# Two state space scans inside a 12-stage network on one core: another order of the steps within a scan round

## The chip, the cores and the metric

One core of a Trainium2 chip runs the whole program. The metric is the device time of one execution in microseconds (us), the median of a few runs. The engines are TensorE (PE in the profile; its weight loads are PEld), VectorE (DVE), ScalarE (ACT), GpSimd (POOL) and SyncE (SP, which only issues transfers). Each engine runs its own list of instructions strictly in the order in which the program issues them, and waits on semaphores where it needs another engine's result.

## The reference, cut to what matters

The network has 12 stages over 1024 tokens of width 256. Two of them are state space blocks ("Mamba 2"); the larger one, `ssd3`, has 64 heads of 64 channels and the smaller, `ssd2`, 8 heads. Cut to its core:

```
proj = hidden @ in_proj_w                       # x, gate z, B, C, dt
x, B, C = silu(causal_conv4(proj_xBC))          # 4 taps per channel
cum   = cumsum(dt * A)
decay = exp(mask(cum_i - cum_j))
scores = (C_i . B_j) * decay * dt_j
Y_diag = scores @ x
state  = chunk_decay * state + B^T (decay_to_end * dt * x)
Y_off  = (C @ state) * exp(cum)
y = (Y_diag + Y_off + D * x) * silu(z)
out = (y * rsqrt(mean(y*y) + eps) * norm_w) @ out_proj_w
```

## The kernel before

The kernel is one program in which each engine walks through the same list of steps, `order[si]`, stage by stage, and issues of every step only its own part. For the two scan stages `ssd_order` writes that list. The work of a scan stage is cut into units. A job is a group of 8 heads (512 channels) with one of two sequences; a job has 4 units, one for each chunk of 128 tokens. So `ssd3` has 16 jobs and 64 units, and `ssd2` has 2 jobs and 8 units. The list is software pipelined: in round r each step of the tuple `ROUND` (L2378) handles unit n = r - lag. Rounds run from -9 to N + 8. Steps such as `silu`, `scan`, `xd` and `scale` come once in 4 rounds. The change is in the order of that tuple alone, so it alters the order inside a round on each engine.

What the steps that matter here do, and on which engine (n is the unit):

- `wo` (lag 3): TensorE, 8 matmuls 128x256, the output projection; `add`: VectorE adds it to `yacc`.
- `E` (lag 0): TensorE, two matmuls that use strips of 32 rows of the array (the exponents' strip products), and, for three chunks in four, the full-array product `EC`. `decay`: ScalarE takes Abs of both `E` banks, Exp of the tile, and Exp of `EC`. `mask`: VectorE multiplies the tile with the masked C.B products.
- `S` (lag 1): TensorE, the products `off` (8 matmuls 128x128) and `S` (2 of 128x512). `state`: VectorE reads both.
- `y` (lag 1): TensorE, 16 matmuls into strips of 64 columns (the outputs' strip products); it needs the masked tile of its unit. `merge`: VectorE adds the result.
- `conv` and `z` (lag -7): TensorE, 6 matmuls 128x512 each, the two input projections. For `conv`, ScalarE copies the bank with one tap and VectorE adds three taps; for `z`, ScalarE copies the bank.
- `xt` and `xt0`: TensorE, 4 transposes, and ScalarE's copy of them. `xt` runs in three rounds out of four, `xt0` in one.
- `scan` (lag -5, once in 4 rounds): ScalarE writes `dA4` in two small copies, TensorE multiplies it (2 matmuls 128x128, bank `cumT`), ScalarE reads the bank three times, then VectorE and GpSimd go on.
- `silu` (lag -3, once in 4 rounds): ScalarE, two passes over 128x2048. `split` (lag -8): ScalarE and VectorE split the next weights, in every second job. `square`, `gate`, `sum`, `keep`, `x`: ScalarE (square) and GpSimd.

PSUM has 8 banks of 128x512 f32. `Psum.take` deals them out in the order in which TensorE takes them: bank k is the one that was taken 8 takes earlier, and TensorE first waits for that one's last reader. So the order of the tuple also decides whose reader each take waits for. The takes are `wo` 1, `E` 2, `EC` 1, `cumT` 1, `off` 1, `S` 1, `conv` 1, `y` 1, `z` 1, `xt` or `xt0` 1. A round has 8 to 11 of them.

A round is named here by r modulo 4, as r0, r1, r2 and r3. `silu` comes in r1, `xt0` in r2 (where the normal `xt` comes too), `scan` in r3, `xd` (4 scalings of the converted tile on ScalarE) in r0. r0 has no `EC` and no `S`; r1 has no `off` and no `xt`.

Lines: L79 is `Engine.mm`, L83 `Engine.tr`, L87 `Engine.act`, L91 `Engine.tt`, L99 `Engine.stt`, L111 `Engine.copy`; all of them are helpers, so groups are told apart by tiles and shapes. All buffers of the scan are cut from the large tiles `wt`, `work`, `ering`.

Of the kernel before, what the change touches and what calls it, by code (L numbers as in the profile page):

```python
# [200 lines left out]
def build(nc, D, out):  # L201
    ctx = ExitStack()
    with ctx:
# [2171 lines left out]
        SSD["ssd3"] = ssd_buffers("ssd3", 4096, 64)  # L2375
        s_xz, s_wo = [sig(f"xz_in{i}") for i in range(8)], [sig(f"wo_in{i}") for i in range(2)]

        ROUND = (("add", 3), ("wo", 3), ("E", 0), ("gate", 2), ("state", 1), ("x", 0), ("scan", -5), ("keep", 0), ("S", 1), ("xt0", -2), ("decay", 0), ("merge", 1), ("conv", -7), ("silu", -3), ("split", -8), ("scale", -1), ("sum", 2), ("square", 2), ("y", 1), ("z", -7), ("mask", 0), ("xd", 0), ("xt", -3))  # L2378
        LEAD = {-9: [("dt",), ("softplus",), ("bc", 0, 0), ("dA",)], -8: [("bc", 1, 0), ("bc", 0, 1)],
                -7: [("cum",)], -5: [("ready",)], -4: [("bc", 1, 1)], 0: [("bc", 0, 2), ("bc", 1, 2)]}  # L2380

        def ssd_order(si):
# [11 lines left out]
            for r in range(-9, N + 9):  # L2394
                todo.extend(LEAD.get(r, ()))
                for step, lag in ROUND:
                    n = r - lag
# [781 lines left out]
```

How the kernel before makes its waits and increments, by code:

```python
    def wait_ge(self, signal, *label):  # L57
        value = signal.at[label] if label and self.sure else signal.at.get(label, 0) if label else signal.n
        if value > self.seen.get(signal, 0):
            self.seen[signal] = value
            self.e.wait_ge(signal.sem, value)
# [103 lines left out]
    def take(self, pe, *key):  # L165
        k = len(self.order)
        b = Bank(k, self.aps[k % 8])
        self.order.append(b)
        self.uses[key] = b
        if k >= 8 and len(self.old) > k:
            assert self.old[k - 8].readers
            for signal, value in self.old[k - 8].readers:
                if value > pe.seen.get(signal, 0):
                    pe.seen[signal] = value
                    pe.e.wait_ge(signal.sem, value)
        return b.ap
# [175 lines left out]
        def need_hT(pe, si, tiles):  # L352
            for t in tiles:
                pe.wait_ge(hT_by(t), "hT", si, t)
# [1 line left out]
        def v_norm(v, step, si, t):  # L356
            if step == "na":
                if si:
                    v.wait_ge(V, "X", si - 1, t)
                else:
                    v.wait_ge(s_x, "X", t // HALF)
                v.bn(lst[:, t, :], X[:, t, :]).then_inc(V)
                v.wait_ge(V)
                v.bn_end(lmv[:, t, :], lst[:, t, :]).then_inc(V, "mv", si, t)
            elif step == "nb":
                v.wait_ge(A, "sd", si, t)
# [20 lines left out]
        def pe_norm(pe, step, si, t):  # L387
            if step == "turn":
                b = ps.take(pe, "turn", si, t)
                pe.wait_ge(V, "H", si, t)
                for c in range(2):
```

## Time and profile before

| what | value |
|---|---|
| median of 3 runs | 1964.95 us (1962.99 to 1966.03) |
| span of the profiled execution | 1943.9 us |
| outside the span (median less span) | 21.05 us |
| PE busy in the span | 1691.9 us (87%) |
| DVE busy | 1457.5 us (75%) |
| ACT busy | 1222.1 us (63%) |
| POOL busy | 891.9 us (46%) |
| mean granted TensorE clock | 0.926 of full speed |

The span runs from the first to the last instruction. The page gives no separate device time for the profiled execution; the difference to the median of the runs, 21.05 us, is what lies around the span and is taken as constant. `ssd2` lies between about 900 and 985 us of the span and `ssd3` between about 1195 and 1808 us. Inside `ssd3` the full rounds, in which all steps are present, lie between about 1270 and 1740 us.

### The profile page before, as it was taken

The page shows a single profiled execution, that of the slowest core. Times are in us where ns is not written, and L with a number is a line of the kernel's source. Part 1 is how long each engine was busy: PE and PEld are TensorE (multiplying, and loading weights), DVE is VectorE, ACT ScalarE, POOL GpSimd, SP SyncE. Part 2 cuts the span into 40 slices and gives each one's busy share as a digit, 9 for nine tenths or more (in the row PEclk, how much of TensorE's full clock was granted, in tenths as well). Part 3 has the DMA queues.
Part 4 walks back from the last instruction along what each step waited for, and adds up shares of the span by engine and source line. Part 5 has one row for each costly group of instructions (what it writes and reads, how often), then busy time and mean ns, then how long its engine had stood idle before and what let it go on. Part 6 is the DMA issues. An engine that isn't in the chain of part 4 may idle for free. (4 is left out here: it accounts for less than half of the span.)

```text
span 1943.9 us, 29621 instructions
## 1 busy us (share of the span) xinstructions
PE 1691.9 (87%) x10866; PEld 1350.1 (69%) x10866; DVE 1457.5 (75%) x3045; ACT 1222.1 (63%) x2463; POOL 891.9 (46%) x870
## 2 busy tenths in 40 slices
PE   6899579979994667798878998899999999997899
PEld 4799257858992356696667886667777777775788
DVE  7888687577886766686677667678788888877576
ACT  4587247646871269317932544888988989887443
POOL 0775541107856300301722220267788787878321
PEclk9999789989996779798989998999999999999799
DMA  8797214117973100000020100000100000000111
GB/s 306 230 294 241 66 55 150 51 35 235 295 228 92 60 1 2 1 1 0 1 97 1 37 30 1 23 12 22 34 17 23 28 23 20 25 14 1 45 49 36
DMA packets 74605, 139.86 MB, mean 72 GB/s; under 512 B 11476, under 2 KB 52564, under 8 KB 73428
## 3 DMA queue, kind: packets, MB, share of 16 engines
q1 hardware_dynamic: 63700, 108.50, 16.9%
q0 software_dynamic: 10752, 29.37, 5.3%
q8 instruction: 89, 1.46, 0.3%
q14 instruction: 64, 0.52, 0.1%
HBM read 113.72 MB, written 24.12 MB: 71 GB/s over the span
## 5 line engine op out<-in xcount | busy, mean ns | idle before, releaser
L79 PE MATMUL ps<-H_r,wt_r 128*128 128x512 f32 (+1 forms) x732 | 284.6, 429 | 11.7 <-ACT wt L87 4.7
L79 PE MATMUL ps<-work_r 128*128 128x256 f32 (+2 forms) x1200 | 248.0, 297 | 6.7 <-DVE work_r L91 2.6
L87 ACT ACTIVATE work<-ps 128x512 f32<-128x512 f32 (+3 forms) x354 | 168.1, 498 | 120.4 <-PE ps L79 103.3
L91 DVE TENSOR_TENSOR work<-work,ps 128x512 f32<-128x512 f32 (+4 forms) x304 | 170.7, 562 | 90.9 <-ACT work L87 57.6
L79 PE MATMUL ps<-wt,work 128*128 128x256 f32 (+1 forms) x1120 | 221.0, 372 | 20.4 <-POOL work L91 10.0
L99 DVE SCALAR_TENSOR_TENSOR wt<-ps,wt 128x511 f32<-128x511 f32 (+2 forms) x234 | 174.3, 747 | 47.2 <-ACT wt L87 41.1
L79 PEld LDWEIGHTS ps<-work_r 128*128 128x128 f32 (+1 forms) x1200 | 189.8, 187 | 28.6 <-DVE work_r L91 11.4
L79 PEld LDWEIGHTS ps<-wt,work 128*128 128x128 f32 (+1 forms) x1120 | 168.4, 201 | 44.6 <-ACT work L87 10.0
L79 PEld LDWEIGHTS ps<-H_r,wt_r 128*128 128x128 f32 (+1 forms) x732 | 139.8, 191 | 63.0 <-issue 14.5
L91 POOL TENSOR_TENSOR work<-work 128x256 f32<-128x256 f32 (+2 forms) x160 | 131.8, 827 | 108.1 <-ACT work L87 87.6
L87 ACT ACT_TABLE_LOAD x113 | 145.0, 1283 | 47.7 <-DVE lmv L119 29.2
L79 PE MATMUL ps<-hT_r,wt_r 128*128 128x512 f32 (+1 forms) x432 | 172.6, 400 | 0.0
L79 PE MATMUL ps<-ering_r,work_r 128*128 128x256 f32 (+1 forms) x742 | 163.5, 301 | 0.9 <-ACT work L87 0.9
L145 POOL DMA_INDIRECT work<-Hd,work x128 | 123.4, 964 | 88.4 <-DVE work L123 58.3
L79 PE MATMUL ps<-ering,work 128*64 128x128 f32 (+2 forms) x1600 | 149.9, 288 | 7.8 <-DVE ering L91 4.0
L79 PEld LDWEIGHTS ps<-ering,work 128*64 128x64 f32 (+1 forms) x1600 | 124.9, 155 | 44.6 <-issue 18.5
L87 ACT ACTIVATE work_r<-work 48x256 fp32r<-48x256 f32 (+1 forms) x200 | 99.1, 495 | 77.8 <-DVE work L91 71.4
L79 PE MATMUL ps<-wt,hT 128*128 128x8 f32 (+4 forms) x384 | 110.4, 433 | 34.3 <-ACT hT L87 17.6
L145 POOL DMA_INDIRECT ering<-ye,get x96 | 94.4, 984 | 92.4 <-DVE X L99 42.2
L91 POOL TENSOR_TENSOR work<-wt,work 128x512 f32<-128x512 f32 x112 | 134.7, 1220 | 0.0
L87 ACT ACTIVATE wt<-wt 128x512 f32<-128x512 f32 (+4 forms) x152 | 132.1, 934 | 2.5 <-DVE wt L99 2.2
L99 DVE SCALAR_TENSOR_TENSOR X<-ps,work,X 128x256 f32<-128x256 f32 x256 | 114.4, 478 | 18.2 <-PE ps L79 11.6
(255 smaller groups left out, 4203.0 us busy)
## 6 DMA issues: line engine op xcount, KB each, us to landing
ering<-in_moe_w SPq DMA_DIRECT2D x87, 624.0 KB, 5.8
ye<-work SPq DMA_DIRECT2D x64, 256.0 KB, 4.6
wt<-in_ssd_wg SPq DMA_DIRECT2D x64, 128.0 KB, 2.2
ye<-early SPq DMA_DIRECT2D x1, 4096.0 KB, 14.6
wt<-in_ssd_wg SPq DMA_DIRECT2D x8, 512.0 KB, 3.6
Hd<-H SPq DMA_DIRECT2D x16, 128.0 KB, 1.7
wt<-in_ret_fc SPq DMA_DIRECT2D x2, 1024.0 KB, 11.7
work<-Hd,work POOLq DMA_INDIRECT x128, 4.8
```

The lines of the kernel that those rows point to most:

```text
L79: self.last = self.e.matmul(o, l, r, start=start, stop=stop, skip_group_check=True)
L87: self.last = self.e.activation(o, a, f, **kw)
L91: self.last = self.e.tensor_tensor(o, a, b, op)
L99: self.last = self.e.scalar_tensor_tensor(out=o, in0=a, scalar=s, in1=b, op0=op0, op1=op1, **kw)
L145: self.last = self.e.indirect_dma_start(out=out, out_offset=at(out_off), in_=in_, in_offset=at(in_off))
```

## The change

One tuple is reordered; no step, lag, instruction or transfer is added or taken away.

```diff
--- before.py
+++ after.py
@@ -2375,7 +2375,7 @@
-        ROUND = (("add", 3), ("wo", 3), ("E", 0), ("gate", 2), ("state", 1), ("x", 0), ("scan", -5), ("keep", 0), ("S", 1), ("xt0", -2), ("decay", 0), ("merge", 1), ("conv", -7), ("silu", -3), ("split", -8), ("scale", -1), ("sum", 2), ("square", 2), ("y", 1), ("z", -7), ("mask", 0), ("xd", 0), ("xt", -3))
+        ROUND = (("wo", 3), ("gate", 2), ("x", 0), ("scan", -5), ("keep", 0), ("S", 1), ("xt0", -2), ("add", 3), ("state", 1), ("y", 1), ("square", 2), ("E", 0), ("merge", 1), ("decay", 0), ("mask", 0), ("conv", -7), ("silu", -3), ("split", -8), ("scale", -1), ("sum", 2), ("z", -7), ("xd", 0), ("xt", -3))
```

Read engine by engine, the order in a round becomes:

| engine | before | after |
|---|---|---|
| TensorE | wo, E, EC, scan, off, S, xt0, conv, y, z, xt | wo, scan, off, S, xt0, y, E, EC, conv, z, xt |
| ScalarE | scan, xt0, decay, conv, silu, split, scale, square, z, xd, xt | scan, xt0, square, decay, conv, silu, split, scale, z, xd, xt |
| VectorE | add, state, scan, merge, conv, split, mask | scan, add, state, merge, mask, conv, split |
| GpSimd | gate, x, scan, keep, sum | gate, x, scan, keep, sum |
| SyncE | transfers after conv and z, after wo | the same |

## Rows read from the trace of the kernel before

**Rows 1.** Windows view, full rounds of `ssd3`: length, busy time per engine, granted clock, DMA.
```profile
1270.00:1750.00 480.00, 472.25 (x2830) 344.77 (x2828) 396.69 (x541) 424.18 (x690) 376.25 (x378) 1.00 0.08 22
```

**Rows 2.** Timeline of PE, one round r2: start, busy, engine, line, operation, tiles, count.
```profile
1400.33 1.89 PE L79 MATMUL ps<-wt,work 128*128 128x256 f32 x8
1402.15 0.50 PE L79 MATMUL ps<-ering_r,wt_r 32*128 32x512 f32 x2
1402.58 0.50 PE L79 MATMUL ps<-work_r 128*128 128x512 f32 x1
1402.91 1.05 PE L79 MATMUL ps<-ering,work 128*128 128x128 f32 x8
1403.80 1.02 PE L79 MATMUL ps<-work,ering 128*128 128x512 f32 x2
...
1405.79 0.50 PE L79 MATMUL ps<-H_r,wt_r 128*128 128x512 f32 x1 [0.53 <-ACT wt L87]
...
1407.59 1.09 PE L79 MATMUL ps<-ering,work 128*64 128x128 f32 x16
1408.61 0.50 PE L79 MATMUL ps<-H_r,wt_r 128*128 128x512 f32 x1
1408.95 0.40 PE L79 MATMUL ps<-hT_r,wt_r 128*128 128x512 f32 x1
...
1410.11 0.60 PE L83 MATMUL ps<-cst,wt 128*128 128x128 f32 x4
1410.54 0.81 PE L79 MATMUL ps<-wt,work 128*128 128x256 f32 x3
```

**Rows 3.** Timeline of PE, two sequences rare before: S then y, y then E.
```profile
930.54 1.97 PE L79 MATMUL ps<-ering,work 128*64 128x128 f32 x16 [2.65 <-DVE ering L91]
932.44 0.79 PE L79 MATMUL ps<-ering_r,wt_r 32*128 32x512 f32 x2
...
1741.35 1.02 PE L79 MATMUL ps<-work,ering 128*128 128x512 f32 x2
1742.30 1.09 PE L79 MATMUL ps<-ering,work 128*64 128x128 f32 x16
```

**Rows 4.** Timeline of PE, landmarks: z of r0 thrice, E, scan of r3, E.
```profile
1356.49 0.50 PE L79 MATMUL ps<-H_r,wt_r 128*128 128x512 f32 x1
...
1390.63 0.50 PE L79 MATMUL ps<-H_r,wt_r 128*128 128x512 f32 x1
...
1394.41 0.50 PE L79 MATMUL ps<-ering_r,wt_r 32*128 32x512 f32 x2
...
1413.26 0.46 PE L79 MATMUL ps<-cst,work 128*128 128x128 f32 x2
...
1421.57 0.49 PE L79 MATMUL ps<-ering_r,work_r 32*128 32x512 f32 x2
...
1425.75 0.50 PE L79 MATMUL ps<-H_r,wt_r 128*128 128x512 f32 x1
```

**Rows 5.** Timeline of ACT: decay of r1, dA4 of r3, in two jobs, and between.
```profile
1361.61 1.07 ACT L87 ACTIVATE ering<-ps 128x512 f32<-128x512 f32 x2
...
1377.32 0.42 ACT L87 ACTIVATE work<-work 128x64 f32<-128x64 f32 x2
...
1395.78 1.08 ACT L87 ACTIVATE ering<-ps 128x512 f32<-128x512 f32 x2
...
1404.64 0.61 ACT L87 ACTIVATE work<-work 128x512 f32<-128x512 f32 x1
1405.17 1.06 ACT L87 ACTIVATE wt<-ps 128x512 f32<-128x512 f32 x2
...
1412.70 0.41 ACT L87 ACTIVATE work<-work 128x64 f32<-128x64 f32 x2
...
1422.09 1.08 ACT L87 ACTIVATE ering<-ps 128x512 f32<-128x512 f32 x2 [1.50 <-PE ps L79]
```

**Rows 6.** Timeline of DVE, the three taps of one `conv`.
```profile
1375.98 2.32 DVE L99 SCALAR_TENSOR_TENSOR wt<-ps,wt 128x511 f32<-128x511 f32 x3 [1.55 <-ACT wt L87]
```

## The prediction

> **What bounds the kernel now.** I read the windows view first, because the change touches only the scan stages. In the 480 us of full rounds TensorE is busy 472.25 us, at full clock, while ScalarE has 424.18 us and VectorE 396.69 us [rows 1]. So TensorE is the bound on average, with ScalarE 12% behind it. The average does not say how the slack is spread, so I then read the PE timeline of one round, measuring from the start of one group to the start of the next [rows 2], and last the ACT timeline over a whole job of four rounds [rows 4, 5].
>
> The PE timeline shows two kinds of loss. The first is paid at each passage between full-array products and strips. In [rows 2] `wo` to `E` takes 1.82: eight matmuls at 0.216 (seven of them lie between 1400.33 and the last start, 1.89 less its own 0.38) would make 1.73, so entering strips costs 0.09. Leaving the `y` strips costs 0.10 before `z` (`y` to `z` takes 1.02) and another 0.10 inside `z`: its first matmul is followed after 0.34, the others at 0.232 ((1410.11 - 1408.95) / 5), so `z` takes 1.50, where six at 0.232 are 1.39.
>
> The second loss is a true wait: `conv` of r2 starts at 1405.79 after 0.53 idle, released by ScalarE [rows 2]. It takes the bank of `z` of r1, eight takes back, and ScalarE copies that bank only at 1405.17, behind `silu` [rows 5]. ScalarE is saturated over this stretch: from Abs of r1 at 1395.78 to `dA4` at 1412.70 its operations follow each other, and the scan product starts at 1413.26, 0.56 after `dA4` [rows 4, 5]. The `E` of that r1 had been issued at 1394.41, 1.37 before ScalarE came to it: before the change ScalarE does not wait for `E` in r1. It does wait in r0, 1.50 us for the `E` issued at 1421.57 [rows 4, 5].
>
> **The change, part by part.** No instruction comes or goes, so only passages and waits count.
>
> *Passages.* `E` now follows `y`, not `wo`: minus 0.09. `z` now follows `conv`, not `y`: minus 0.20. The passage from `y` strips to `E` strips is new. The nearest case is at half clock, where `E` starts 0.07 before the end shown for the 16 `y` matmuls (930.54 + 1.97 against 932.44) [rows 3]; `z` behind `y` at full clock also starts 0.07 before it (1407.59 + 1.09 against 1408.61) [rows 2]. So I charge the same 0.10; bounds 0 to 0.20. `S` to `y` takes 0.95 [rows 3], which is 2 x 0.43 plus the 0.09 that `conv` to `y` paid before. Net per full round: -0.19 us, 56 rounds: -10.6 us, if TensorE alone set the pace.
>
> *ScalarE's chain.* It starts `decay` of r1 only when `E` is there, and `E` now comes later in the round, behind `S` and `y`. I count from the start of `z` in r0. TensorE needs `z` 1.39 + `xt` 0.43 + `wo` 1.73 + `S` 0.95 + `y` 1.02 = 5.52 to `E` [rows 2, 3]; Abs starts 0.52 after it (1422.09 - 1421.57) [rows 4, 5]: 6.04. Before, Abs of r1 started 5.15 after `z` (1395.78 - 1390.63). ScalarE loses 0.89, in which it now does one `square` (0.52, from 1404.64 to 1405.17) that formerly stood later.
>
> From Abs to the scan product the chain was 17.48 (1413.26 - 1395.78) in a job with `split`; less that `square` it is 16.96. In a job without `split` ScalarE needed 15.71 (1377.32 - 1361.61) to `dA4`, plus 0.56 less 0.52: 15.75 [rows 4, 5]. TensorE by itself would need about 14.3 from `E` of r1 to the scan product of r3: `E`, `EC`, `conv`, `z` 3.55; in r2 `wo`, `off`, `S` and transposes 3.48, strip entry and `y` 1.6, `E`, `EC`, `conv`, `z`, `xt` 3.98; `wo` 1.73 [rows 2, 3]. ScalarE's chain is 0.52 + 16.96 = 17.5 or 16.3. So TensorE, which formerly had another `y` and another `E` with `EC` in this stretch, waits 2 to 3 us in it: about 1 us at `EC` of r2, which now takes the bank of `z` of r1 (eight takes back), and up to 2 us at the scan product. Behind that waiting product are `off`, `S`, `y` and `E` of r3, so all of the round shifts; a wait at `EC` itself is followed by `conv` and `z`.
>
> *From the scan product to the next `z` of r0*, TensorE runs in its own time; ScalarE is idle before both `decay` steps there. In the new order: scan 0.30, `off` 0.89, `S` 0.95, `y` 1.02, `E` 0.43, `EC` 0.34, `conv` 1.39, `z` 1.39, `xt` 0.43, `wo` 1.73, `off` with strip entry 0.98, `y` 1.02, `E` 0.43, `conv` behind strips 1.49, together 12.79 [rows 2, 3, 4].
>
> *Sum of one job.* With `split` 6.04 + 16.96 + 12.79 = 35.79, against 35.12 before (1425.75 - 1390.63): +0.67. Without, 6.04 + 15.75 + 12.79 = 34.58, against 34.14 (1390.63 - 1356.49): +0.44 [rows 4]. There are 14 such periods, 7 of each kind: **+7.8 us**. If `y` to `E` is free, `E` of r1 comes 0.10 earlier and the last stretch is 0.20 shorter: +3.6. If it costs 0.20: +12.
>
> *VectorE.* `mask` moves ahead of the taps, so it idles behind `merge` until Exp is done, with the taps (2.32) [rows 6] and `split` queued behind. The bank takes that wait for taps are `EC` of r1 and the second `E` bank of r2; followed through the job, taps end about 0.8 us before either. `y` needs `mask` one round later and has some 2 us left. I charge 0.
> *GpSimd and SyncE* keep their order; transfers are issued behind the same steps. 0.
>
> *Fill and end of both scans.* Without `conv` and `z`, `E` stands behind `off`, `S` and `y`, 0.89 + 0.95 + 1.02 = 2.86 later in its round, and `square` stands before `decay` in the chain of the last rounds, 0.52 each in some three rounds per scan. Bounds: 0, if ScalarE is busy anyway, as in r1 before; 2 x 2.86 if the last `E` of both scans is late in full. I take +2.
>
> **Forecast.** Span 1943.9 + 7.8 + 2 = 1953.7; with the 21.05 around it 1974.8, say **1975 us**, 0.5% slower. Its own range is 1969 to 1981.
>
> **The rivals.** *Passages win.* If ScalarE keeps ahead after all, the -10.6 stand and the time is 1954. For it speaks that TensorE is 98% busy [rows 1]. Against it: it requires the chain from Abs of r1 to the scan product to be 2 to 3 us shorter than it was, and nothing is taken out of it but one `square`. The Trainium skill, TensorEngine Tiling (Array Packing), section Tiling Modes, says that changing the tiling mode drains the engine; by that rule three changes of mode a round in place of four are a gain, and the page gives no figure. By it alone the time would be this rival's. Chance 0.15.
>
> *The two cancel.* ScalarE's lag is half of what I count, for instance because `E` of r1 comes before ScalarE is free there, as before the change. The chain is then 0.5 us shorter per period, and with it goes the end of the stages: +7.8 - 14 x 0.5 = about +1, 1966. Chance 0.2.
>
> *VectorE becomes a second wait.* If `mask` in front of the taps makes them miss the 0.8 us that I find, each period gets a wait of 1 to 2.3 us (the taps themselves [rows 6]) at a bank: +14 to +32 instead of the chain's share, 1983 to 1997. It decides if taps start over 0.8 us later than the mask's end allows. Chance 0.1.
>
> The main case has 0.55. The waits could also lower the clock; the granted clock was 1.00 through the waits before [rows 1], so I give that no share of its own.
>
> **How the numbers follow.** About 0.2% (3.9 us) is what a measurement of this kernel can tell from no change. Slower: nearly all of 0.55 and all of 0.1, 0.62. Same: 0.2 and the low end of the main case, 0.23. Faster: 0.15. The range 1955 to 1985 reaches from the passages' rival to the near end of VectorE's; it holds the main case and the cancelling one.
>
> **What would show it.** In the changed profile: `y` to `E` in 1.02 and `conv` to `z` in 1.39 (passages right); Abs of r1 waiting for TensorE, which it did not before; a wait of about 1 us at `EC` of r2 and one of 1.5 to 2 us at the scan product of r3, both released by ScalarE; ScalarE without idle time between; jobs of 35.8 and 34.6 us. PE busy in the full rounds falls from 98% to about 93%, and the clock stays at full speed. The forecast is wrong if ScalarE is not late at the scan product, or if the long waits are released by VectorE.

## The result and the profile after

| | median | against the kernel before, same chip |
|---|---|---|
| before | 1965.49 us (1962.99 to 1969.46, 4 runs) | |
| changed | 1988.53 us (1984.98 to 1991.76, 4 runs) | 1.0115, 95% interval 1.0102 to 1.0128 |
| changed, second time | 1988.6 us (5 runs; before 1968.64) | 1.0104, 1.0086 to 1.0122 |

The change costs 1.0 to 1.15%, 20 to 23 us. The forecast was 1975, so the sign is right and the size is half of the truth; the time lies above the range.

The windows view of the changed kernel shows its `ssd2`, the 14 full jobs of `ssd3`, a job with `split` and one without (columns as in [rows 1]):

```profile
895.70:1027.20 131.50, 107.10 (x547) 80.21 (x548) 87.30 (x161) 93.47 (x171) 55.81 (x57) 0.84 0.00 1
1279.61:1780.77 501.16, 460.35 (x2827) 349.98 (x2826) 398.33 (x544) 430.67 (x701) 373.81 (x376) 1.00 0.07 20
1351.36:1388.27 36.91, 33.23 (x204) 25.18 (x203) 29.69 (x42) 31.76 (x53) 27.26 (x27) 1.00 0.07 22
1388.27:1422.83 34.56, 32.95 (x205) 25.19 (x203) 26.62 (x37) 29.55 (x48) 26.06 (x27) 1.00 0.09 24
```

The same view of the kernel before, over its `ssd2` and its 14 full jobs:

```profile
871.70:999.20 127.50, 103.48 (x548) 76.39 (x548) 85.90 (x161) 93.74 (x171) 54.88 (x57) 0.88 0.00 1
1250.93:1736.80 485.87, 474.14 (x2828) 345.70 (x2826) 397.66 (x543) 431.35 (x702) 372.12 (x375) 1.00 0.07 21
```

TensorE is busy 14 us less in the same matmuls, and the stretch is 15.3 us longer: cheaper passages, and more waiting than they save. (The clock is full in both but for one stretch of 3.40 us in the first of the 14 jobs before the change, where it is at 0.50 with TensorE busy throughout; by an estimate from that row, 1.7 us of the 14 are this.) ScalarE, VectorE and GpSimd do the same work in the same time to 2 us. A job without `split` takes 34.56 (34.58 predicted), one with `split` 36.91 (35.79 predicted). The whole miss inside `ssd3` is in the jobs with `split`.

The PE timeline of that job and the next, at the places where TensorE waits (columns as in [rows 2]):

```profile
1355.85 1.09 PE L79 MATMUL ps<-ering,work 128*64 128x128 f32 x16
1356.87 0.50 PE L79 MATMUL ps<-ering_r,wt_r 32*128 32x512 f32 x2
1357.31 0.50 PE L79 MATMUL ps<-work_r 128*128 128x512 f32 x1
...
1366.91 0.50 PE L79 MATMUL ps<-work_r 128*128 128x512 f32 x1 [0.72 <-ACT wt L87]
...
1374.38 0.46 PE L79 MATMUL ps<-cst,work 128*128 128x128 f32 x2 [1.62 <-ACT work L87]
...
1385.22 0.49 PE L79 MATMUL ps<-ering_r,work_r 32*128 32x512 f32 x2
1386.81 0.47 PE L79 MATMUL ps<-H_r,wt_r 128*128 128x512 f32 x1 [1.10 <-DVE wt_r L91]
...
1410.05 0.46 PE L79 MATMUL ps<-cst,work 128*128 128x128 f32 x2 [1.43 <-DVE wt L99]
```

The first three rows are the new sequence `y`, `E`, `EC`: 1.02 and 0.44. Then come `EC` of r2, the scan product of r3, `E` and `conv` of r0, and the scan product of the next job. The first two waits are forecast. The third is not: `conv` of r0 starts 1.59 after `E` (1386.81 against 1385.22), where the natural distance is 0.43. (The releaser named at 1410.05 is the last one by the record; that the `dA4` copies hold it is shown by `d_after` below.)

Where this wait comes from is best seen in the chain of waits, followed back from `z` of that r0 (start, time, engine and tile):

```profile
1374.38 3.71 PE ps L79 x30
1378.09 1.08 ACT ering L87 x2
1379.17 0.02 issue
1379.20 1.07 ACT ering L87
1380.27 0.02 issue
1380.29 2.02 DVE ering L91
1382.31 0.67 DVE wt L99
...
1384.53 2.14 DVE wt_r L91 x2
1386.67 0.14 issue
1386.81 2.99 PE ps L79 x12
```

From the scan product the path runs through `off`, `S`, `y`, `E`, then Abs, Exp, `mask`, the taps and the two `split` operations, and only then `conv`. `conv` of r0 needs the weights that `split` of r3 writes. This is a data wait (`pe.wait_ge(V, "split", ...)`), not a bank. Before the change `mask` was last in its round. The DVE and PE timelines of the kernel before, `split` of r3 and `conv` of r0:

```profile
1421.73 1.29 DVE L91 TENSOR_TENSOR wt_r<-wt,wt_r 128x256 fp32r<-128x256 f32 x2
```
```profile
1423.17 0.47 PE L79 MATMUL ps<-H_r,wt_r 128*128 128x512 f32 x1
```

`split` ended at 1423.02 and `conv` began 0.15 later. That is already some 0.2 us late: from scan product to `conv` it took 9.91 us in this job (1413.26 to 1423.17) and 9.68 in the one without `split` ahead of it (1378.36 to 1388.04). So this wait stood in the trace before, with no slack left, and could have been read there.

The grouped DVE view (1270 to 1740 us) shows where VectorE now stands: group, count, busy, mean ns, idle before. First the changed kernel, then the kernel before:

```profile
L91 DVE TENSOR_TENSOR ering<-ering 128x1024 f32<-128x1024 f32 x52 | 83.4, 1604 | 63.9 <-ACT ering L87 63.9
```
```profile
L91 DVE TENSOR_TENSOR ering<-ering 128x1024 f32<-128x1024 f32 x55 | 84.0, 1528 | 0.0
```

VectorE now stands idle for 63.9 us in front of `mask`, and for none before the change. All that follows `mask` in its list starts that much later.

The stages, between the same matmuls (by their number) in each trace, in us:

| kernel | `ssd2` | `ssd3` fill | full rounds | end |
|---|---|---|---|---|
| before | 127.5 | 58.7 | 488.6 | 98.1 |
| changed | 131.5 | 59.4 | 503.8 | 97.1 |
| changed, second time | 134.2 | 58.6 | 503.7 | 98.6 |
| `d_after` | 128.0 | 56.8 | 485.2 | 96.2 |
| `d_after_split` | 127.9 | 56.8 | 476.9 | 97.2 |
| `b_mix` | 122.9 | 54.0 | 479.2 | 99.1 |
| `d_before` | 122.8 | 53.7 | 490.4 | 96.2 |
| `c_gscan` | 131.6 | 59.5 | 496.7 | 95.7 |

Everything between the two scans and behind them is alike to 1.2 us. The stretch ahead of `ssd2` took 871.7 us in the profile of before and 891 to 897 in these others, but 871 to 875 in the first four experiments below, taken on a chip on which the kernel before runs in 1946.6. So it goes with the chip and not with the change.

### The profile page after: what moved, and what is told of

Read it like the earlier page. It is cut to its first block and busy times, and to the rows that moved or that the text cites. A ratio compares the mean times of both kernels' runs of the same rounds, so it can differ in the third digit from the quotient of the medians.

```text
span 1987.5 us, 29653 instructions
## 1 busy us (share of the span) xinstructions
PE 1694.8 (85%) x10866; PEld 1366.9 (69%) x10866; DVE 1457.4 (73%) x3045; ACT 1221.9 (61%) x2463; POOL 891.5 (45%) x870
## 3 DMA queue, kind: packets, MB, share of 16 engines
q8 instruction: 90, 1.47, 0.3%
## 5 line engine op out<-in xcount | busy, mean ns | idle before, releaser
L79 PE MATMUL ps<-H_r,wt_r 128*128 128x512 f32 (+1 forms) x732 | 259.0, 406 | 15.4 <-DVE wt_r L91 11.7
L91 DVE TENSOR_TENSOR ering<-ering 128x1024 f32<-128x1024 f32 (+4 forms) x90 | 119.5, 1328 | 103.9 <-ACT ering L87 103.4
L91 POOL TENSOR_TENSOR work<-work 128x256 f32<-128x256 f32 (+2 forms) x160 | 143.1, 900 | 72.8 <-DVE work L91 30.7
L87 ACT ACTIVATE work_r<-work 48x256 fp32r<-48x256 f32 (+1 forms) x200 | 99.1, 496 | 80.0 <-DVE work L91 73.5
L79 PE MATMUL ps<-wt,hT 128*128 128x8 f32 (+4 forms) x384 | 111.0, 434 | 37.7 <-DVE hT L111 13.9
L87 ACT ACTIVATE lrs<-lmv,epsc 128x1 f32<-128x1 f32 x96 | 27.8, 294 | 172.1 <-DVE lmv L119 136.2
## 6 DMA issues: line engine op xcount, KB each, us to landing
wt<-in_ssd_wg SPq DMA_DIRECT2D x64, 128.0 KB, 2.2
Hd<-H SPq DMA_DIRECT2D x16, 128.0 KB, 1.7
```

Source lines behind the costliest of these rows:

```text
L79: self.last = self.e.matmul(o, l, r, start=start, stop=stop, skip_group_check=True)
L87: self.last = self.e.activation(o, a, f, **kw)
L91: self.last = self.e.tensor_tensor(o, a, b, op)
```

## The experiments

My theory after the first result: two lags cause the loss. ScalarE is late at the scan product of r3 in every job (as forecast), and VectorE is late at `conv` of r0 in the jobs with `split`, because `mask`, which waits for the late `E`, stands ahead of the taps and `split`. The rivals: the late `E` alone, or the clock. All edits are to the changed kernel unless said. Where an expectation gives a time, it is meant for a chip on which the kernel before takes 1965.5 us; the first four runs are from a faster one, and there the ratio is what compares.

**`e_front`: `E` back behind `wo`, all else in the new order.**

```diff
-ROUND = (("wo", 3), ("gate", 2), ... ("square", 2), ("E", 0), ("merge", 1), ...
+ROUND = (("wo", 3), ("E", 0), ("gate", 2), ... ("square", 2), ("merge", 1), ...
```

> The changed kernel with one step put back: E and EC stand behind wo again (y stays ahead of conv, mask stays ahead of the taps). My theory: what costs time is that E comes late, because ScalarE's decay and VectorE's mask wait for it. Then a job without split takes 34.1 us and one with split 34.7 to 35.1, and the time is 1961 to 1967 us, level with the kernel before. The rival, that y ahead of conv (its bank now comes from z of the round before, its mask is needed earlier) is what costs: the time stays at 1983 or more.

Measured: 1954.59 against 1946.62, ratio 1.0033 (1.0019 to 1.0047), some 15 us better than the change. By the ratio it is 1972 us where 1961 to 1967 were expected. Jobs of 35.1 and 34.5: the waits at the scan product and at `conv` of r0 are gone, and the split job is back at its old time. The job without `split`, expected at its old 34.1, is 0.4 above it: `y` of r2 waits 0.32 for the bank of `z` of r1 and `wo` of r3 0.35, both released by ScalarE (0.90 and 0.36 in a job with `split`). The place of `E` carries most of the loss.

**`e_mask_back`: `mask` behind `z`, as it was.**

```diff
-... ("decay", 0), ("mask", 0), ("conv", -7), ... ("z", -7), ("xd", 0), ...
+... ("decay", 0), ("conv", -7), ... ("z", -7), ("mask", 0), ("xd", 0), ...
```

> The changed kernel with mask put back to the end of VectorE's round, behind conv's taps and split. My theory of the second loss is that split on VectorE stands behind mask, and conv of r0 waits for split of r3. Then that wait of about 1.1 us in jobs with split goes away (scan product to next z of r0 12.8 us instead of 13.9). But y stands early now and needs mask: I expect y to wait 0.5 to 1 us in r0 and r1 of each job and up to 4 us in r2 of jobs with split, so 1990 to 2010 us in all. The rival, that mask ahead of the taps is pure loss: 1980 or less.

Measured: 2048.7, ratio 1.0511 (1.049 to 1.0533), which is 2066 us by the ratio: far above the 1990 to 2010 expected. Jobs of 36.2 and 46 us. PE timeline, `y` in two neighbouring rounds:

```profile
1435.71 1.09 PE L79 MATMUL ps<-ering,work 128*64 128x128 f32 x16 [1.67 <-DVE ering L91]
...
1448.21 1.73 PE L79 MATMUL ps<-ering,work 128*64 128x128 f32 x16 [3.63 <-DVE ering L91]
```

With `y` early in the round, `mask` cannot stand late: `y` waits for it, and the late `y` makes the next `E` and so the next `mask` late. The expectation had the direction; it missed that the waits feed each other and that the clock falls too. The granted clock over the 14 jobs is 0.93 (1.00 in the changed kernel), and the second `y` above takes 1.73 in place of 1.09. From scan product to `z` the jobs take 14.3 and 18 to 19, not the 12.8 expected, so this run does not show what the wait for `split` is worth. It does show that the early `mask` is not an avoidable part of the change.

**`e_split_first`: `split` ahead of `decay` and `mask`.**

```diff
-... ("merge", 1), ("decay", 0), ("mask", 0), ("conv", -7), ("silu", -3), ("split", -8), ...
+... ("merge", 1), ("split", -8), ("decay", 0), ("mask", 0), ("conv", -7), ("silu", -3), ...
```

> The changed kernel with split moved ahead of decay on ScalarE and so ahead of mask on VectorE. My theory: VectorE's split is then done while it would idle before mask, the wait at conv of r0 in jobs with split goes (13.9 to 12.8 us), and one split (0.6 us) leaves ScalarE's chain between Abs of r1 and the scan product: jobs with split fall from 37.0 to 35.3 us, jobs without stay at 34.6. 7 x 1.7 = 12 us less than the changed kernel: 1975 to 1979 us. The rival, that the 1.1 us comes from a bank (taps of r3) and not from split: at most 0.6 us a job is gained, 1984 us.

Measured: 1961.97, ratio 1.0068 (1.0052 to 1.0084). The first two split jobs take 35.78 and 35.23, with 12.78 and 12.77 from scan product to `z`: the wait at `conv` is gone. They were expected at 35.3; from the third on they take 37.2 again, for another reason. PE timeline and windows of such a place:

```profile
1491.24 0.46 PE L79 MATMUL ps<-cst,work 128*128 128x128 f32 x2 [2.08 <-ACT work L87]
1491.54 1.23 PE L79 MATMUL ps<-ering,work 128*128 128x128 f32 x8
1492.56 1.92 PE L79 MATMUL ps<-work,ering 128*128 128x512 f32 x2
1494.41 1.70 PE L79 MATMUL ps<-ering,work 128*64 128x128 f32 x16
```
```profile
1485.00:1492.29 7.29, 5.21 (x30) 4.30 (x29) 4.56 (x6) 6.62 (x15) 3.82 (x5) 1.00 0.00 0
1492.29:1495.70 3.41, 3.41 (x17) 1.91 (x18) 2.66 (x6) 1.55 (x5) 0.00 (x0) 0.50 0.00 0
```

`split` now stands ahead of `decay` on ScalarE, the scan product waits 2.08 in place of 1.62, and behind it the granted clock is at 0.50 (1.2 GHz) for 3.41 us. This happens in the last five split jobs, with waits of 2.04 to 2.08; the second one waits 2.04 too and keeps its clock. In the changed kernel, with 1.6 in six split jobs and 1.9 in the first, it stays at 1.00 through all jobs. The rival that put the split jobs' loss on the clock is out for the changed kernel, but the clock is what ate this experiment's gain: its 14 jobs take 499.1 us, 2.0 less than with the change. By the ratio the time is 1979 us, at the end of the 1975 to 1979 expected, but not by the mechanism expected: the jobs fall by 2 us of the 12, and the medians, taken on two chips, differ by 7 to 9. Differences of this size between the two chips I leave open.

**`o_ssd2`: the new order in `ssd2` alone, the old in `ssd3`.**

```diff
-for step, lag in ROUND:
+for step, lag in (NEW if q.key == "ssd2" else OLD):
```

> The new order in the small scan stage alone, the old order in the large one. From the two traces I read 4 us for the small stage and 15 for the large one: 1969 to 1970 us. If the small stage's share is an accident of the two profiled executions: 1965 to 1966 us.

Measured: 1949.98, ratio 1.0019 (1.0005 to 1.0033): 3.7 us. `ssd2` goes from 127.5 to 131.4, as expected. The 14 full jobs of `ssd3`, in the old order, take 487.8 in place of 485.9: in four of the split jobs `conv` of r0 waits 0.3 for `split`, which takes 1.61 there where it takes 1.28 in a job without this wait, and they take 35.38 in place of 35.04. So the wait for `split` can show in the old order too, only smaller. PE timeline of the changed kernel in `ssd2`:

```profile
979.07 1.09 PE L79 MATMUL ps<-ering,work 128*64 128x128 f32 x16 [1.05 <-DVE ering L91]
...
986.64 1.09 PE L79 MATMUL ps<-ering,work 128*64 128x128 f32 x16 [1.51 <-DVE ering L107]
...
1002.90 1.09 PE L79 MATMUL ps<-ering,work 128*64 128x128 f32 x16 [1.85 <-DVE lrs L107]
```

Each of these starts 0.09 to 0.15 after the end of a `mask` (978.92, 986.49 and 1002.81); the short operations named as releasers in the last two follow `mask` on VectorE. With no `conv` and `z` left to run in the meantime, `y` stands behind `E`, Exp and `mask` in full.

**`r_after` and `r_before`: ScalarE relieved.** Both leave out the `silu` of z, one of the two 1.9 us passes of r1 (the gate then multiplies with z itself); one on the new order, one on the old.

```diff
-a.act(q.sz[j % q.nx], q.sz[j % q.nx], ACT.Silu).then_inc(A, "sz", si, j)
+a.mark("sz", si, j)
```

> The changed order with ScalarE relieved: the silu of the gate z is left out (the gate multiplies with z itself), so one pass of 1.8 us is gone from ScalarE's chain of every job. My theory: the chain from Abs of r1 to the scan product sets the pace in the changed order, so its jobs shrink by most of 1.8 us: without split from 34.6 to 32.8 us, with split from 37.0 to 35.3 us. About 16 x 1.75 = 28 us less than the changed kernel: 1960 us. The rival, that TensorE or VectorE sets it: jobs stay within 0.4 us, 1983 or more.

> The same relief in the order of before. There TensorE is near its own limit (waits of about 0.7 us a job without split, 1.2 with), so only 0.5 to 1.1 us a job can be had: 33.5 and 34.2 us, in all 1950 to 1957 us. With both relieved, the order with fewer passages should come out level or ahead in jobs without split: 32.8 against 33.5 us. The rival, that passages are worth nothing in the full round: both jobs alike.

Measured: 0.9988 (0.9976 to 1.0) on the old order, and 1.0012 (0.9999 to 1.0026) on the new, which without it has 1.0104 to 1.0115. Two microseconds less on ScalarE per job are worth some 20 us in the new order and 2 in the old: ScalarE has become the limit there. Both sizes were missed. On the new order 1960 us was expected and 1968 came: the job without `split` gained 0.9 (33.65) and not 1.8, and ScalarE now idles 0.33 twice in its r2 for TensorE, at `xt0` and at `E`. On the old order 33.5 and 34.2 were expected, and the jobs stayed at 34.1 and 35.1 to 35.6. With both relieved, the new order is ahead by 0.5 in the jobs without `split`. Of the 20 us, some 4 or 5 are not ScalarE's but come from the split jobs described next.

The split jobs of `r_after` held a surprise. From scan product to `z` four of the last six take 12.77 and two 13.9 to 14.0. Windows of a short one and of a long one:

```profile
1438.70:1451.49 12.79, 12.79 (x88) 10.02 (x89) 11.84 (x20) 7.67 (x16) 9.61 (x10) 1.00 0.00 1
1575.76:1589.78 14.02, 12.83 (x88) 10.02 (x88) 13.17 (x19) 9.04 (x17) 10.82 (x12) 1.00 0.01 2
```

Then `mask`, `split` and the GpSimd operation beside `mask`, from the timelines of DVE and of POOL, first of the short one, then of the long one:

```profile
1444.62 1.23 DVE L91 TENSOR_TENSOR ering<-ering 128x1024 f32<-128x1024 f32 x1 [0.64 <-ACT ering L87]
...
1448.01 1.01 DVE L91 TENSOR_TENSOR wt_r<-wt,wt_r 128x256 fp32r<-128x256 f32 x2
...
1581.68 2.12 DVE L91 TENSOR_TENSOR ering<-ering 128x1024 f32<-128x1024 f32 x1 [0.64 <-ACT ering L87]
...
1585.94 2.22 DVE L91 TENSOR_TENSOR wt_r<-wt,wt_r 128x256 fp32r<-128x256 f32 x2
```
```profile
1444.63 2.11 POOL L91 TENSOR_TENSOR ering_r<-wt,work_r 128x512 fp32r<-128x512 f32 x1
...
1581.68 1.04 POOL L91 TENSOR_TENSOR ering_r<-wt,work_r 128x512 fp32r<-128x512 f32 x1
```

In the short one `mask` starts 0.01 ahead of GpSimd's multiply and takes 1.23, while the multiply takes 2.11. In the long one the multiply takes 1.04 and `mask` 2.12. One of the two pays about the time of the other. So it is in all 14 such places of this profile: in the four where `mask` starts at least 0.01 ahead it takes 1.23 and the multiply 2.07 to 2.11; in the other ten, from level to 0.11 behind, `mask` takes 2.02 to 2.12 and the multiply 1.04. The pair in the long one costs 2.1 us more on the path to `conv`; in the changed kernel `mask` and `split` have 2.02 and 2.21 in this place, the long form. The Trainium skill, SBUF — State Buffer, section SBUF: two separate sides, says that VectorE and GpSimd share a pair of ports under an exclusive lock, held for the whole instruction by whichever starts first, and that a VectorE operation with two SBUF inputs takes it against a GpSimd operation that reads SBUF. The rows agree, to the 0.01 that the starts tell: the loser is longer by 0.8 to 1.1, and VectorE's operations of 128x512 that read a bank keep their 0.67 to 0.69 beside a busy GpSimd.

**`d_after` and `d_before`: the scan product's input early.** The two `dA4` copies become a step of their own in r0, three rounds ahead of the product, in the new order and in the old.

```diff
-... ("y", 1), ("square", 2), ...
+... ("y", 1), ("dA4", -8), ("square", 2), ...
-            elif step == "scan":
+            elif step == "dA4":
                 four = q.dA[:, 4 * b_:4 * b_ + 4, g * 8:g * 8 + 8]
...
+            elif step == "scan":
                 b, sc = ps.of("cumT", si, j), wts["scan_c"]
```

> The changed order, with ScalarE's two small copies to dA4 moved four rounds of work earlier (lag -8, in r0, where ScalarE idles) out of the scan step. The scan product then no longer ends ScalarE's chain. My theory: its wait of 1.5 to 2 us in r3 goes, what stays is the wait at EC of r2 (0.4 to 1 us): jobs without split 33.1 us, with split 35.4 us, so about 1965 us. The rival, that the product waits for its bank or for VectorE: no change, 1985 or more.

> The same early dA4 in the order of before. There the scan product waited only 0.15 to 0.2 us beyond what the bank of conv (taps of r2) costs anyway: 0 to 2 us less in all, 1963 to 1965 us.

Measured: 0.9973 (0.9964 to 0.9983) on the new order, 26 to 28 us better than the change (18.6 of it in the 14 full jobs, 482.5 us); 0.9946 (0.993 to 0.9963) on the old. Windows of `d_before`, its 14 jobs:

```profile
1265.55:1753.16 487.61, 473.82 (x2828) 345.54 (x2826) 399.86 (x543) 430.77 (x702) 372.24 (x376) 1.00 0.07 21
```
Windows of `d_after`, a job with `split` and one without:

```profile
1411.03:1446.86 35.83, 33.28 (x205) 25.35 (x203) 30.77 (x43) 31.92 (x53) 29.61 (x30) 1.00 0.08 23
1446.86:1480.06 33.20, 32.98 (x204) 25.26 (x203) 26.13 (x37) 29.25 (x48) 26.30 (x28) 1.00 0.09 24
```

Without the wait at the scan product the job without `split` is 0.94 shorter than before the change (34.14): here the passages are cashed. The split job still waits 1.28 at `conv` of r0 for `split` (33.1 and 35.4 were expected). On the old order 0 to 2 us were expected; by the median it is 8 and by the ratio 11. It is not in the full jobs (34.12 and 35.05 to 35.38) but in `ssd2` (122.8 in place of 127.5) and in the fill of `ssd3` (53.7 for 58.7); why the two starts profit so much stays open. What matters below: the early input is worth 0.5% to the old order as well, so it is `d_before`, and not the kernel before, that the new order with early input has to beat.

**`d_after_split`: both, and `a_again`: the changed kernel on the same chip.**

> The changed order, with the two dA4 copies ahead of square in r3 and split ahead of decay. Theory (ScalarE's lag makes the scan product late, and the taps and the split standing behind mask make conv of r0 late): with both taken away the jobs keep what the passages give, 33.2 us without split and about 34.0 to 34.4 with it, against 34.15 and 35.06 of the kernel before; the changed order alone has 34.57 and 37.0. From d_after (33.2 and 35.8) the seven split jobs fall by 1.4 to 1.8 us, 10 to 12 us in all: 1 to 1.5% faster than the changed order and 0.8 to 1.1% faster than the kernel before. Rival (the split jobs lose to the clock or to ScalarE's total, not to the order of split): they stay at 35.8, and the time at d_after's 0.997 of before.

(The copies stand in r0, as in `d_after`; the expectation says r3 by mistake.)

> The changed kernel unaltered, on the same chip as the other three, so that they can be set against it: 1.0115 of the kernel before if the ratio holds from chip to chip (1.010 to 1.013). If it came out under 1.009 or above 1.014, the ratios of the other runs would have to be compared with it and not with the first result.

Measured: 1953.31 against 1968.64, 0.993 (0.9914 to 0.9946); `a_again` 1.0104 (1.0086 to 1.0122), within what was expected. For `d_after_split` 0.8 to 1.1% faster than before was expected; it is 0.7%. Windows of `d_after_split`, 14 jobs, one with `split`, one without:

```profile
1270.51:1744.78 474.27, 458.75 (x2827) 350.74 (x2826) 391.82 (x544) 426.91 (x697) 375.03 (x376) 1.00 0.08 22
1338.09:1372.40 34.31, 33.02 (x204) 25.27 (x203) 28.76 (x41) 31.02 (x52) 27.48 (x28) 1.00 0.08 23
1372.40:1405.59 33.19, 32.98 (x205) 25.27 (x203) 25.99 (x37) 29.65 (x50) 26.62 (x28) 1.00 0.09 25
```

The 14 jobs take 474.3 us, 11.6 less than before the change and 26.9 less than with it. Of the 11.6, 2.0 are in the first of them, the one that held the stretch at half clock before. The other thirteen gain 9.6, about 1.0 each without `split` and 0.4 to 0.5 with it, so the same matmul order gains about what [rows 2, 3] said the passages are worth, once the waits for ScalarE and VectorE are short. The split jobs settle at 34.6, since `conv` of r0 now waits 0.60 for the taps. In `ssd2` it still loses 5 us against `d_before` (127.9 against 122.8), so in the whole it is ahead of it by only 3 us by the ratios (0.993 against 0.9946, and the intervals overlap) and 4 by the stages.

**`b_silu`: on top of that, the `silu` of z behind the copy of z.**

```diff
+... ("z", -7), ("siluz", -3), ("xd", 0), ...
```

> As d_after_split, and the second silu pass (that of z) stands behind ScalarE's copy of z in r1, not ahead of it. Theory: the copy of z of r1 frees its bank about 3.9 us earlier, so EC of r2 no longer waits (0.2 us in a job without split, 0.8 with it in the changed order), and nothing else moves: 0.2 to 0.8 us per job, 3 to 9 us in all below d_after_split. Rival: TensorE has no wait left at EC once dA4 is early, and the pass is only moved onto the xt copy behind it: within 0.1% of d_after_split.

Measured: 0.9935 (0.9919 to 0.995), no different from `d_after_split`; the jobs are the same 33.2 and 34.6. The rival had it.

**`b_mix`: that order in `ssd3`, the old one with early `dA4` in `ssd2`.**

> ssd3 in d_after_split's order, ssd2 in the old order with the early dA4. Theory: ssd2 is short of conv and z to cover mask, so there the new order costs about 4 to 5 us (131.5 against 127.5; 128.0 against 122.8 with the early dA4) while in ssd3 it gains: about 5 us below d_after_split, 1.0 to 1.3% below the kernel before. Rival (the ssd2 difference was a difference between chips): equal to d_after_split within 0.1%.

Measured: 1945.76, 0.9889 (0.9872 to 0.9905), 1.1% faster than the kernel before, as expected, and the best of all. `ssd2` takes 122.9 in place of 127.9. Against `d_before` (0.9946) it is 11 us ahead by the ratios, and as much in the 14 jobs of `ssd3` (476.5 against 487.6): this is what the new order with `split` ahead of `decay` is worth. No run has early copies and early `split` in the old order, so the share of `split`'s new place is not shown; in the jobs without `split`, 34.12 against 33.20, it has none.

**`c_gscan`: GpSimd's multiplies of the scan out of the way.** They move from r3 to the end of r0; the PE, ACT and DVE lists are those of the changed kernel.

```diff
-... ("sum", 2), ("z", -7), ...
+... ("sum", 2), ("gscan", -4), ("z", -7), ...
-            elif step == "scan":        # g_unit
+            elif step == "gscan":
```

> The changed order, with GpSimd's three multiplies of the scan (128x256 and two 128x512) moved from r3 to the end of r0, so that in the split jobs GpSimd does not run them while VectorE's mask of r3 and its two split operations want to run. All of the data that conv of r0 waits for comes as late as before. Theory (the wait of 1.16 us at conv of r0 comes from the overlap: mask takes 2.02 us and the split pair 2.21 us there, against 1.22 and 1.01 where they run alone): mask of r3 under 1.8 us, split near 1.0, conv of r0 waits under 0.3 us, split jobs 35.8 to 36.1 instead of 37.0, no-split jobs 34.6, together 6 to 8 us or 0.3 to 0.4% below the changed kernel. Rival (the wait is the late E and Exp alone, whatever the durations): conv of r0 still waits about 1.1 us and split jobs stay at 37.0. A third outcome, that GpSimd's other operations move up into the same place and overlap as much, would show as mask and split still near 2 us, and would leave the question open.

Measured: 1980.09 against 1966.97, 1.0076 (1.0055 to 1.0097), 5 to 8 us below the changed kernel (7.1 in the 14 jobs), where 6 to 8 were expected. The split jobs take 35.92, and from scan product to `z` 12.76 us. DVE timeline, `mask` and `split` of r3, then PE at `conv` of r0:

```profile
1445.73 1.76 DVE L91 TENSOR_TENSOR ering<-ering 128x1024 f32<-128x1024 f32 x1 [0.71 <-ACT ering L87]
...
1449.64 1.33 DVE L91 TENSOR_TENSOR wt_r<-wt,wt_r 128x256 fp32r<-128x256 f32 x2
```
```profile
1450.66 0.49 PE L79 MATMUL ps<-ering_r,work_r 32*128 32x512 f32 x2
1451.12 0.47 PE L79 MATMUL ps<-H_r,wt_r 128*128 128x512 f32 x1
```

The pair takes 3.09 in place of 4.23, and `conv` follows `E` after 0.46: no wait. `E` comes as late as before. So the late `E` alone does not make the wait; it takes the late `E` and the overlap with GpSimd together. The pair did not fall to its shortest times (1.23 and 1.01 in `r_after`), since other multiplies of GpSimd moved up beside it, and `split` ends just in time (1450.97).

**`c_mix`: the same in `b_mix`.**

> As b_mix (ssd3 in the changed order with early dA4 copies and split ahead of decay, ssd2 in the old order with early dA4 copies), and in ssd3 GpSimd's scan multiplies at the end of r0. In the best order so far conv of r0 in a split job still waits 0.66 us for the taps, with mask at 1.48 and split at 1.34. Theory of the overlap: mask 1.2 to 1.3, split 1.0, the wait falls under 0.3 us, split jobs 34.2 instead of 34.6: 2 to 4 us below b_mix, 1.2 to 1.3% below the kernel before. Rival: equal to b_mix within 0.1%, 1.1% below the kernel before.

Measured: 0.9949 (0.9932 to 0.9967), 0.6% slower than `b_mix`. Both theory and rival missed. There `split` stands ahead of `mask`, and GpSimd's next two steps, moved up, fall on both: 1.84 and 2.06 in place of 1.34 and 1.48, and the split jobs take 14.7 from scan product to `z` (13.8 in `b_mix`). The jobs without `split` lose too (33.6 for 33.2). The overlap was not removed but moved.

## Why the prediction was right in sign and wrong in size

**Passages: right.** `y` to `E` takes 1.02 as charged. In a job without `split` the change is worth 0.94 us (34.14 to 33.20) where the scan product does not wait (0.87 of it in the busy time of TensorE, 33.85 to 32.98), 0.22 to 0.23 a round against the 0.19 forecast. The Trainium skill's rule that a change of tiling mode drains TensorE (TensorEngine Tiling (Array Packing), section Tiling Modes) has the sign of this right; the rival that rested on it fell by the waits.

**ScalarE's chain: right.** From `z` of r0 to the scan product 21.78 and 23.02 (1351.36 to 1374.38) were measured, where 21.79 and 23.00 had been worked out. Abs of r1 was to wait for TensorE: ScalarE idles 0.43 before it without `split`, but only 0.06 with it (`square` ends at 1357.35, Abs starts at 1357.41), so there both are late at once. The wait at the product was forecast at 1.5 to 2 and is 1.62 and 1.43, the one at `EC` of r2 at 1 and is 0.72 with `split` (0.2 without). The clock stayed full. Busy TensorE is 92% (460.35 of 501.16) for the 93% forecast.

**VectorE: the step that failed, "I charge 0".** I followed the taps to the banks that wait for them, and they are in time. I missed the other reader of VectorE's list: `split` stands behind the taps, and `conv` of r0 waits for its data. The last stretch is 12.78 without `split` (12.79 forecast) and 13.89 with it (1374.38 to 1388.27). That is 1.1 us in six split jobs and 0.8 in the first, 7.5 us, as much as the whole loss forecast for the jobs (7.8). The slack fails with it: before the change `mask` and `split` took 1.47 and 1.29 in this place, and beside GpSimd's multiplies of the scan they take 2.02 and 2.21. `c_gscan` shows that with 3.09 for the pair the charge of 0 would have held. So the missing reader alone would not have changed the forecast: with the durations read before the change `split` would have been in time. The charge fails by the reader and the longer durations together, and the overlap with GpSimd was nowhere in the prediction, which put GpSimd at 0 because its order does not change. The rival on VectorE named the right engine with the wrong mechanism (taps at a bank, in each period) and gave 1983 to 1997; that the 1988.5 lie in its range is luck.

**Fill and end: mis-sized.** I took +2 for both scans. `ssd2` costs 4.0 in the first profile and 6.7 in the second, 3.7 by the runs of `o_ssd2`; the fill and end of `ssd3` cost nothing (156.5 against 156.8). So the sum is 15.3 + 4 to 7, 19 to 22 us, against 20 to 23 by the medians.

**Outside the span.** The 21.05 us are not around the span: in a later run the profiled execution took 1988.6 with a span of 1986.7. So about 2 us are around the span, and the rest goes with the chip ahead of `ssd2`: the profile before fits the faster one. The forecast adds differences only, so this did not move it.

## What to carry to other kernels

When a step that waits is moved ahead of others on an in-order engine, list every consumer of what now stands behind it, data waits as well as buffers, and look in the trace before the change for those that already have no slack. Put that slack against VectorE's durations beside a busy GpSimd in the new order, not against those of the old one. Here the two together cost as much as the effect that was found. A new order of the matmuls can be sound while the lists of the helpers are not: the same PE order lost 1.1% as it was, and stood 0.7% ahead of the kernel before once the input of the scan product and `split` were issued ahead of what waits. But give every repair to the old order too before you credit the new one: the early input alone gave the old order 0.5%, and the new order is worth its place in `ssd3` only, 11 us there, and costs 5 in `ssd2`.

## What was not expected of the hardware

- Which of VectorE and GpSimd starts first, by about 0.01 us, decides who pays: `mask` 1.23 and multiply 2.11, or `mask` 2.12 and multiply 1.04, in one and the same kernel, and with it 1.1 us of a job.
- A wait of 2.04 to 2.08 us at the same place was followed by 3.41 us at half the clock in five of six split jobs; with waits of 1.6 to 1.9 us there the clock stayed at full speed. That the length of the wait decides this is not shown.
